# Softmax over the heads: the second sum of the heads as an accumulating DMA, and the weighing split eleven heads to five

## The reference, cut to what matters

```python
q = (x @ Wq.T + bq).reshape(B, S, H, D)      # B 4, S 1024, H 16, D 8
k = (x @ Wk.T + bk).reshape(B, S, H, D)
v = (x @ Wv.T + bv).reshape(B, S, H, D)
scores = jnp.einsum('bqnd,bknd->bnqk', q, k) / jnp.sqrt(jnp.float32(D))
attn = jax.nn.softmax(scores, axis=1)        # axis 1: the heads
out = jnp.einsum('bnqk,bknd->bqnd', attn, v).reshape(B, S, E)
return out @ Wo.T + bo
```

## Time and profile before

| | us |
|---|---|
| median of 3 runs | 2010.51 (2009.56 to 2012.01) |
| the profiled execution's own time | 2014.26 |
| its span, from the first to the last instruction | 2012.4 |
| head softmax stage, first to last sum of the heads (L840) | 553.33 to 1691.92 |

### The profile page before, as it was taken

One profiled execution on the slowest core, in us unless ns is written; L12 is line 12 of the kernel. 1 busy time (PEld: TensorE's weight loads), 2 busy tenths in 40 slices (PEclk: granted clock), 3 DMA queues, 4 the chain that ended last, 5 costly groups with the idle time before them and its releaser, 6 DMA issues. The chain is left out here.

```text
span 2012.4 us, 54448 instructions
## 1 busy us (share of the span) xinstructions
PE 1915.1 (95%) x21688; PEld 1273.7 (63%) x21688; DVE 1715.0 (85%) x2601; ACT 1241.3 (62%) x2217; POOL 1547.4 (77%) x1180
## 2 busy tenths in 40 slices
PE   5998899999699999999999999999999998999998
PEld 3666644444367777777777777777777776544443
DVE  6776688886689999999999999999999997788876
ACT  4566456666466666666666666666666665566665
POOL 5255365656199999999999999999999997556565
PEclk8999799999799999999999999999999999799999
DMA  6744278564400000000000000000000000587762
GB/s 162 196 101 96 48 140 152 132 127 86 140 13 14 10 17 10 14 14 11 17 10 14 14 12 16 10 14 14 8 8 6 10 6 2 100 156 152 126 139 52
DMA packets 119886, 118.97 MB, mean 59 GB/s; under 512 B 50641, under 2 KB 82273, under 8 KB 118897
## 3 DMA queue, kind: packets, MB, share of 16 engines
q1 hardware_dynamic: 114112, 112.89, 25.9%
q10 hardware_dynamic: 5520, 2.60, 0.5%
HBM read 96.95 MB, written 18.55 MB: 57 GB/s over the span
## 5 line engine op out<-in xcount | busy, mean ns | idle before, releaser
L1099 DVE TENSOR_REDUCE head_shift<-head_score 128x64 bf16<-128x1024 f32 x512 | 624.1, 1219 | 81.8 <-PE head_score L883 69.8
L1056 ACT ACTIVATE head_ex<-head_score 128x1024 f32<-128x1024 f32 x512 | 524.7, 1025 | 185.3 <-PE head_score L905 183.5
L840 POOL TENSOR_TENSOR head_half<-head_ex 128x1024 f32<-128x1024 f32 x256 | 604.8, 2363 | 40.6 <-ACT head_ex L1056 40.6
L1355 POOL TENSOR_TENSOR ffn_sw<-ffn_sg,ffn_wide 128x512 f32<-128x512 f32 x256 | 325.0, 1269 | 218.7 <-ACT ffn_sg L1466 203.3
L1106 DVE TENSOR_TENSOR head_ex<-head_ex,head_recp 128x1536 f32<-128x1536 f32 x256 | 446.7, 1745 | 5.2 <-ACT head_recp L1028 5.2
L915 PE MATMUL head_den<-head_half,c_ident 128*128 128x128 f32 x3072 | 387.3, 276 | 2.5 <-POOL head_half L841 2.5
L915 PEld LDWEIGHTS head_den<-head_half,c_ident 128*128 128x128 f32 x3072 | 365.1, 193 | 6.0 <-POOL head_half L841 2.6
L847 POOL TENSOR_TENSOR head_ex<-head_ex,head_recip 128x512 f32<-128x512 f32 x256 | 329.0, 1285 | 22.6 <-ACT head_recip L1030 14.6
L905 PE MATMUL head_score<-head_shift,c_identb 128*128 128x512 bf16 x1024 | 310.0, 384 | 18.0 <-DVE head_shift L1099 12.0
L883 PE MATMUL head_score<-att_b_HB,att_b_GR 96*128 96x256 f16 x2048 | 311.5, 274 | 0.5 <-ACT head_ex L1056 0.5
L898 PE MATMUL head_outp<-head_ex,att_b_vs 128*32 128x128 f32 x8192 | 277.1, 276 | 0.0
(11 more groups left out here) (264 smaller groups left out, 2468.3 us busy)
## 6 DMA issues: line engine op xcount, KB each, us to landing
ffn_wide<-pair_weights SPq DMA_DIRECT2D x256, 256.0 KB, 9.7
band_v_windows<-a_values SPq DMA_DIRECT2D x24, 192.0 KB, 4.6
att_b_vs<-in_zero_f SPq DMA_DIRECT2D x2, 2176.0 KB, 10.2
a_keys<-band_parts_k SPq DMA_DIRECT2D x12, 295.5 KB, 2.5
att_a_HB<-a_keys SPq DMA_DIRECT2D x48, 73.9 KB
a_queries<-band_parts_q SPq DMA_DIRECT2D x12, 271.5 KB, 3.0
att_a_GR<-a_queries SPq DMA_DIRECT2D x12, 271.5 KB
b_queries<-head_parts_q SPq DMA_DIRECT2D x32, 96.0 KB, 1.6
```

Source lines behind the costliest of these rows:

```text
L840: ch.link(pool.tensor_tensor(hf, e[:, 0:8, :], e[:, 8:16, :], ALU.add))
L1056: act.activation(ex[:, kt % RING, :, h * QS:(h + 1) * QS], score[:, h, :, :].rearrange("p k (a w) -> p (k a) w", a=NH // 2), ACT.Exp, scal ...
L1099: dve.tensor_reduce(shift[:, h, :], score[:, h, :, :].rearrange("p k (a w) -> p w k a", a=NH // 2), AX.XY, ALU.max, negate=True).then_inc( ...
L1355: pool.tensor_tensor(sw[:, unit % 2, :], sg[:, unit % 2, :], wide[:, k % 2, i, :], ALU.mult).then_inc(sw_ready, 1)
```

## The change

The second sum of the heads leaves POOL's arithmetic and becomes a transfer within SBUF that adds to its destination, issued by POOL: slabs 4 to 7 of `half` are added onto slabs 0 to 3 (2048 bytes on each of 128 partitions, 256 KB). PE then sums four slabs rather than six. The heads in `ex` are stored in another order, so that the split of the weighing can fall anywhere: eleven heads on DVE and five on POOL, where it was twelve and four. The rings grow, and the lag between a unit's exponential and its denominator goes from 2 units to 3. Before it issues a transfer, POOL waits for its own sum (`half_ready`) and for the landing of the transfer before (`quarters_added`).

```diff
-    LAG, RING = 2, 4
-    ON_DVE = 3
-    SLABS = (0, 1, 4, 5, 6, 7)
+    LAG, RING, SUMS = 3, 5, 3
+    ON_DVE = 11
+    SLABS = range(NH // 4)
...
-        half = m.sb("half", [P, 2, NH // 2, P])
+        half = m.sb("half", [P, SUMS, NH // 2, P])
...
+            def sum_heads(unit):
+
+                e, hf = ex[:, unit % RING, :, :], half[:, unit % SUMS, :, :]
                 pool.wait_ge(ex_ready, ONE + 2 * unit + 2)
-                pool.wait_ge(den_ready, ONE + unit)
-                ch.link(pool.tensor_tensor(hf, e[:, 0:8, :], e[:, 8:16, :], ALU.add))
-                pool.tensor_tensor(hf[:, 0:2, :], hf[:, 0:2, :], hf[:, 2:4, :], ALU.add).then_inc(quarter_ready, 1)
+                if unit >= SUMS:
+                    pool.wait_ge(den_ready, ONE + 1 + unit - SUMS + 1)
+                pool.tensor_tensor(hf, e[:, 0:8, :], e[:, 8:16, :], ALU.add).then_inc(half_ready, 1)
+                pool.wait_ge(half_ready, ONE + unit + 1)
+                if unit > 0:
+                    pool.wait_ge(quarters_added, unit * 16)
+                pool.dma_start(hf[:, 0:4, :], hf[:, 4:8, :], accum_op=ALU.add).then_inc(quarters_added, 16)
...
-                e = ex[:, kt % RING, :, :].rearrange("p (g a) q -> p g a q", a=GH)[:, :, ON_DVE, :]
-                pool.tensor_tensor(e, e, recip[:, kt % 2, :][:, None, :].broadcast_to([P, NG, P]),
+                e = ex[:, unit % RING, ON_DVE:NH, :]
+                pool.tensor_tensor(e, e, recip[:, unit % 2, :][:, None, :].broadcast_to([P, NH - ON_DVE, P]),
                                    ALU.mult).then_inc(rest_ready, 1)
...
-                    if i == HH:
+                    if i == ON_DVE:
                         pe.wait_ge(rest_ready, ONE + unit + 2)
...
-                pe.wait_ge(quarter_ready, ONE + unit + 1)
+                pe.wait_ge(quarters_added, (unit + 1) * 16)
...
-                        act.activation(ex[:, kt % RING, :, h * QS:(h + 1) * QS],
-                                       score[:, h, :, :].rearrange("p k (a w) -> p (k a) w", a=NH // 2),
+                        act.activation(ex[:, unit % RING, :, h * QS:(h + 1) * QS].rearrange("p (a g) w -> p g a w", g=NG),
+                                       score[:, h, :, :].rearrange("p k (g a w) -> p (k g) a w", a=GH, w=QS),
...
-                e = ex[:, kt % RING, :, :].rearrange("p (g a) q -> p g a q", a=GH)[:, :, 0:ON_DVE, :]
-                dve.tensor_tensor(e, e, recp[:, 0:P][:, None, None, :].broadcast_to([P, NG, ON_DVE, P]), ALU.mult).then_inc(prob_ready, 1)
+                e = ex[:, unit % RING, 0:ON_DVE, :]
+                dve.tensor_tensor(e, e, recp[:, 0:P][:, None, :].broadcast_to([P, ON_DVE, P]), ALU.mult).then_inc(prob_ready, 1)
```

More of the change, by code:

```diff
@@ L832, in _, with weigh_rest @@
             m.start(pool, "pool")
[L834 to L837 removed]
+            def sum_heads(unit):
+                e, hf = ex[:, unit % RING, :, :], half[:, unit % SUMS, :, :]
                 pool.wait_ge(ex_ready, ONE + 2 * unit + 2)
[L839 to L843 removed]
+                if unit >= SUMS:
[5 more added lines that the diff above has]
+                pool.dma_start(hf[:, 0:4, :], hf[:, 4:8, :], accum_op=ALU.add).then_inc(quarters_added, 16)
+            def weigh_rest(unit):
                 pool.wait_ge(copy_ready, ONE + unit + 1)
[L846 to L847 removed]
+                e = ex[:, unit % RING, ON_DVE:NH, :]
+                pool.tensor_tensor(e, e, recip[:, unit % 2, :][:, None, :].broadcast_to([P, NH - ON_DVE, P]),
                                    ALU.mult).then_inc(rest_ready, 1)
@@ L853, in chunk_of @@
                     if not (first and kt < LAG):
-                        weigh_rest(unit - LAG, (kt - LAG) % BT)
-                    sum_heads(unit, kt)
+                        weigh_rest(unit - LAG)
+                    sum_heads(unit)
             chunk_of(0, True)
@@ L860, in _ @@
             for kt in range(BT - LAG, BT):
-                weigh_rest(LAST * BT + kt, kt)
+                weigh_rest(LAST * BT + kt)
         @block.tensor
@@ L897, in attend @@
                     at = n * VSLOT + VSLOT - D - n4 * D
-                    last = pe.matmul(outp[g * 32:(g + 1) * 32, 0:P], vs[:, buf * BT + kt, at:at + 32], ex[:, kt % RING, n, :],
+                    last = pe.matmul(outp[g * 32:(g + 1) * 32, 0:P], vs[:, buf * BT + kt, at:at + 32], ex[:, unit % RING, i, :],
                                      start=(kt == 0 and n4 == 0), stop=(kt == BT - 1 and n4 == GH - 1), skip_group_check=True)
@@ L908, in take_maximum, with denominator_of @@
                 last.then_inc(shifted, 1)
-            def denominator_of(unit, kt):
-                pe.wait_ge(quarter_ready, ONE + unit + 1)
+            def denominator_of(unit):
+                pe.wait_ge(quarters_added, (unit + 1) * 16)
                 pe.wait_ge(ln_done, ONE + unit)
                 for i, k in enumerate(SLABS):
-                    last = pe.matmul(den[:, 0:P], c["ident"][:, :], half[:, kt % 2, k, :], start=(i == 0), stop=(i == len(SLABS) - 1))
+                    last = pe.matmul(den[:, 0:P], c["ident"][:, :], half[:, unit % SUMS, k, :], start=(i == 0), stop=(i == len(SLABS) - 1))
                 last.then_inc(den_ready, 1)
@@ L952, in chunk_of @@
                     if not (first and kt < LAG):
-                        denominator_of(unit - LAG, (kt - LAG) % BT)
+                        denominator_of(unit - LAG)
                     if kt < BT - 1:
@@ L1019, in high_part, with reciprocal_of @@
                 return act.activation(parts, bank[:, None, :].broadcast_to([P, 2, cols]), ACT.Identity, bias=c["b_bias"][:, u:u + 1])
-            def reciprocal_of(unit, kt):
+            def reciprocal_of(unit):
                 act.wait_ge(copy_ready, ONE + unit)
@@ L1029, in reciprocal_of @@
                 act.wait_ge(rest_ready, ONE + unit)
-                act.activation(recip[:, kt % 2, :], lnd[:, :], ACT.Exp, scale=-1.0).then_inc(copy_ready, 1)
+                act.activation(recip[:, unit % 2, :], lnd[:, :], ACT.Exp, scale=-1.0).then_inc(copy_ready, 1)
             def copy_out(n):
@@ L1061, in chunk_of @@
                         if h == 0 and not (first and kt < LAG):
-                            reciprocal_of(unit - LAG, (kt - LAG) % BT)
+                            reciprocal_of(unit - LAG)
                     ahead(b, q, kt)
@@ L1100, in largest, with weigh @@
                                   AX.XY, ALU.max, negate=True).then_inc(shift_ready, 1)
-            def weigh(unit, kt):
+            def weigh(unit):
                 dve.wait_ge(recip_ready, ONE + unit + 2)
-                e = ex[:, kt % RING, :, :].rearrange("p (g a) q -> p g a q", a=GH)[:, :, 0:ON_DVE, :]
-                dve.tensor_tensor(e, e, recp[:, 0:P][:, None, None, :].broadcast_to([P, NG, ON_DVE, P]), ALU.mult).then_inc(prob_ready, 1)
+                e = ex[:, unit % RING, 0:ON_DVE, :]
+                dve.tensor_tensor(e, e, recp[:, 0:P][:, None, :].broadcast_to([P, ON_DVE, P]), ALU.mult).then_inc(prob_ready, 1)
             def add_output(n):
@@ L1150, in chunk_of @@
                     if not (first and kt < LAG):
-                        weigh(unit - LAG, (kt - LAG) % BT)
+                        weigh(unit - LAG)
                     ahead(b, q, kt)
@@ L1203, in _ @@
             for kt in range(BT - LAG, BT):
[L1204 removed]
+                weigh(LAST * BT + kt)
             stats_of(LAST - 1)
```

8 lines of the change are left out of this document (4 added, 4 removed).

## The result

The changed kernel takes 2185.37 us (median of 4 runs, 2182.56 to 2188.33) beside 2011.03 us for the kernel before in the same comparison. The ratio is 1.0868, with a 95% interval of 1.0849 to 1.0887. The direction was the forecast one; the size was not. 174 us were added where 75 were forecast, and the time lies 10 us above the upper end of the range.

A forecast was written before the change was run, and what follows sets the result against it. Three engines within 6% of the 4.46 us unit bound the kernel, POOL deciding. (4.75 - 4.46) x 252 units gave +73 us, +2 at the end: 2085.5 us, 3.7% slower; range 1960 to 2175 (8 in 10).

The forecast's parts named there:

- That POOL would set the period: After the change POOL's unit, 4.75 us, exceeds PE's 3.95 and DVE's 4.03; chance 0.50 for POOL bound at 2017 to 2200 us.
- PE, VectorE, the five heads: Per unit: PE falls from 4.40 to 3.95 us, DVE from 4.16 to 4.03, POOL's fifth head adds 0.27.
- The unit on POOL is 3.95 + X: POOL's unit: 2.43 for L840 with hand-over, 1.25 for weighing, 0.27 for the fifth head, plus X: 4.75 us.
- X: Time POOL is held issuing the adding transfer once a unit, taken as 0.8 us; break-even at 0.51 us.
- the hand-over from L840 stays: On POOL, the transfer waits for L840 as L841 did, so the 2.43 us from L840's start stay unchanged.
- By the shape [...] the 1.21 us is the nearest row: Upper bound for POOL's issue time, from sixteen SP issues of 256 KB at 1.21 us each in a burst.
- The landing [...] I count nothing: The transfer's landing, 2.5 to 4.1 us, fits in the 4.75 us between POOL's issues, so it costs nothing.
- PE waits for POOL's transfer: Sign to look for: PE's L915, in 8 passes, waiting for POOL's transfer.
- The end of the stage: After the last sum, issue and landing replace L841, less the shorter denominator and L1106: +2 us.
- A short issue: Rival: POOL held only 0.31 to 0.45 us by the issue, unit 4.26 to 4.40 us, 1962 to 1997 us; chance 0.34.
- A landing that sets the period: Rival: the transfer lands later than 4.75 us and becomes the period; 2273 us at 5.5 us; chance 0.07.
- The band for cancelling: Rival: issue time between 0.49 and 0.53 us, so gains and costs cancel, 2006 to 2015 us; chance 0.09.

The follow-up runs named there:

- e1: The changed kernel with 13 heads weighed on VectorE and 3 on GpSimd, issue still ahead of the weighing: 2060.7 us, ratio 1.0238.
- e3: The changed kernel with POOL weighing between its sum and the issue of the adding transfer: 2102.6 us, ratio 1.0449.
- e14: The changed kernel with one adding transfer for two units, issued after the weighing, lag 4, longer rings, split eleven to five: 2025.0 us, ratio 1.0057.
- e2: The changed kernel's rings, lag and head order, but the second sum back on POOL's arithmetic, six slabs, split twelve to four: 2011.6 us, ratio 0.9998.
- e7: The changed kernel with the transfer issued by SP as a plain copy, leaving out the addition: 1946.8 us (one run).
- e6: The changed kernel with POOL's transfer a plain copy, leaving out the addition: 2104.7 us (one run).
- e5: The changed kernel with the transfer adding only slab 4 onto slab 0, 512 instead of 2048 bytes a row: 2175.3 us (one run).
- e12: The changed kernel with the transfer covering only 16 of the 128 rows: 2156.6 us (one run).
- e11: The changed kernel with two semaphores in turn, so POOL waits for the transfer before the last one: 2175.0 us, ratio 1.0807.
- e13: The changed kernel with one adding transfer for two units, issued after the weighing, lag 4, longer rings, split twelve to four: 1992.7 us, ratio 0.9901.
- e4: The changed kernel with the issue after the weighing and 13 heads on VectorE, 3 on GpSimd: 2011.4 us, ratio 0.9998.

## Why the prediction was wrong

- **That POOL would set the period: right.** No idle time ahead of L840 or L850 from 620 to 1600 us, and e1, e3 and e14 move the period by what they take from POOL. The granted clock of PE stayed at 1.00 there.
- **PE, VectorE, the five heads: right.** L918 has 8 passes, 0.89 us from start to start (1100.36 to 1101.25); L1109 takes 1.61 us as worked out; a further head on POOL is 0.27 us. The order of the heads and the longer rings cost nothing (e2).
- **The step that failed: "The unit on POOL is 3.95 + X", with X = 0.8 us and "the hand-over from L840 stays".** In place of the 4.75 us the usual unit is 5.07 and the mean 5.13. The larger part of the miss is the hand-over: to L841 it took 0.08 us, to an issue it takes 0.30, and e3, which takes it away, wins 0.33 us a unit. The issue itself is 0.61 from its start to the next instruction's and 0.29 by which the last part lags and which returns in L840's duration, 0.90 in all, 0.10 over X. The waits for landings and for no shown releaser, taken at nothing, are the last 0.05 to 0.06.
- **X was near by luck.** The middle of a row of SP and a row of ACT says nothing of POOL: SP's issue of this very shape takes 0.46 us (e7), and a copy from POOL 0.60 (e6). The 4.95 us worked out from the 1 us to the first byte, which the Trainium skill gives (DMA: Bandwidth & Descriptors, section Specifications), lie nearer to 5.07, but not for that reason: the issue alone takes 0.88 us, and the hand-over adds the rest.
- **"By the shape [...] the 1.21 us is the nearest row": right as a bound, for another reason.** From 16 to 128 rows and from 512 to 2048 bytes in each the cost hardly moves (e5, e12).
- **"The landing [...] I count nothing": nearly right.** It lands in 3.3 us, but some landings take 5, and e11 prices POOL's wait for them at 10 us. The 2.6 us that the prediction worked out for 256 KB is too low for a transfer that adds; the plain copy lands in 2.3 (e6).
- **"PE waits for POOL's transfer": wrong place.** It waits for the heads that POOL weighs, 166.2 us against 20.2. What is queued behind POOL's issue of unit u is the weighing of unit u - 2, not of u - 3.
- **The end of the stage: +3.8 us for +2.**
- **The sum.** The four misses are 0.10 x 255 = 26 us for the issue, 0.22 x 255 = 56 us for the hand-over, 0.055 x 255 = 14 us for the waits and 2 us at the end: 98 of the 99 us between 174 and 75. The range ended at 2175 with X up to about 1.15; hand-over and waits counted in, the measured 5.13 - 3.95 is 1.18.
- **The rivals.** A short issue is seen only from SP (e7), which is worth 65 us and leaves the addition out; POOL's plain copy (0.60 us, e6) already lies above the 0.51 us at which gain and cost are equal. The floor of 4.1 us was 4.20 in e7. A landing that sets the period did not come. The band for cancelling, 2006 to 2015 us, leaves out the 2 us of the end, which changes nothing.

## What to carry to other kernels

A transfer issued by POOL that adds has a price on POOL that grows far more slowly than its size: 0.79 us for 32 KB in 16 rows, 0.88 for 256 KB in 128 rows, 1.19 for 512 KB in two pieces a row. Where POOL is near the bound, make such issues few and large (e13), and put other work between the instruction that makes the data and the issue (e3). When an instruction on POOL shows a longer duration than the same one elsewhere, compare starts with starts before calling it slower. And with several engines within 6% of the period, the busy time of the next one is a floor that is not reached: 0.14 to 0.16 us a unit over the busy time of the fullest engine stayed in e4, e7 and e13.

## What the runs showed of the hardware that I had not expected

- A POOL instruction's recorded duration can carry the lag of an earlier one: the sum of the heads, 2.36 us by itself, shows 2.65 after one adding issue and up to 3.23 after several when nothing makes POOL wait in between (e3). A plain copy leaves it at 2.36 (e6).
- Adding costs 0.30 us of issue over copying, 64 more packets for each transfer, and 1.0 us more until landing (3.3 for 2.3 us, e6). An adding transfer of 512 KB lands in 5.0 us (e13).
- Nearly all slow landings of POOL's transfers, 29 of 30, come together with a packet of the kind "instruction" on the queue q8. That it delays them is not tested.
- From the end of a sum to an issue that waits for it 0.30 us pass, to an arithmetic instruction 0.08 us.
- 256 KB within SBUF every 4.2 us slowed no instruction of POOL that can be measured (e7).
